# Adjacency build of a four-layer graph kernel: two edge tiles share one accumulator bank and a window of 20 destinations

## Chip, cores and metric

The kernel runs on one core of one Trainium2 chip. The metric is the device time of one execution in microseconds (us). Three runs of the kernel before took 2306.53, 2307.1 and 2308.04 us, median 2307.1 us.

## What is computed

The reference is a stack of four graph layers on 3125 nodes of 128 features. 53125 directed edges (`src`, `dst`) are sorted by destination. The first layer is the one that the change serves: four rounds of "add the neighbours, then a two-layer perceptron".

```python
for l in range(N_LAYERS):                                   # 4 rounds
    agg = jax.ops.segment_sum(x[src], dst, num_segments=n)  # sum over incoming edges
    h = x + agg
    h = jnp.maximum(h @ W1[l] + b1[l], 0.0)
    x = h @ W2[l] + b2[l]
...
x = _layernorm(x + _L0_gnn_ref(x, edge_index, batch0, ...), axis=-1)
x = _layernorm(x + _L1_gnn_ref(x, edge_index, edge_type_8, ...), axis=-1)
x = _layernorm(x + _L2_gnn_ref(x, edge_index, edge_type_16, ...), axis=-1)
x = _layernorm(x + _L3_gnn_ref(x, ..., src, dst, edge_type_8), axis=-1)
```

The other three layers gather rows by edge and sum them by relation; the change does not touch them.

## The kernel before

The kernel has four stages. A setup reads the edge lists and turns them into keys. The **adjacency build** makes a dense matrix `adj` of 128 partitions x 25 blocks x 3136 columns in bf16: row (block h, partition p) is source node 128h + p, a column is a destination, a cell counts edges. The four rounds of the first layer then multiply the node rows by this matrix (line 1320). Three passes with row gathers follow.

The build runs over 416 tiles of 128 edges, in 104 groups of four (`FG` = 4), four groups in a ring of buffers (`FNB` = 4).

- VectorE (DVE) makes for each group one one-hot of the source's place in its block, `flo` (line 2033, 128 x 512 for four tiles), and for each tile one one-hot `foh` (line 2037) of 800 columns: two sub-blocks of 16 destinations, each 25 source blocks x 16.
- TensorE (PE) multiplies the two for each tile, once for either sub-block (lines 1210 and 1212, 400 columns each). The product adds to an accumulator bank of 512 columns in `acc` that belongs to that sub-block of 16 destinations; which bank it is comes from a table read into registers.
- ScalarE (ACT) copies a finished pair of sub-blocks (32 destinations, two banks) into `adj` (line 1713, 128 x 800) and then writes zeros into the two banks (line 1717), since every product only adds. There are 98 pairs and three slots of two banks. How many tiles a pair waits for is data; ACT reads these counts into registers, 12 at a time (line 1719, the loop of line 1726).

The order between the engines is set by semaphores. `foh_ready` counts groups that DVE has made, `fstep_done` tiles that PE has multiplied, `flushed` pairs copied, `zeroed` pairs zeroed. PE waits for `foh_ready` and, by the pair that a group reaches, for `zeroed`; DVE waits for `fstep_done` before it overwrites a buffer; ACT waits for `fstep_done` before a copy and for its own `flushed` before it zeroes. After the build DVE adds the diagonal (lines 2053 and 2058), PE waits for `flushed`, `zeroed` and `diag_set`, and the first round begins (line 1320).

GpSimd (POOL) runs checks and tables in the setup (lines 893 to 931) and nothing during the build. The checks end in one number, `peak`: above 0 the kernel takes a general branch instead of the dense one.

Of the kernel before, what the change touches and what calls it, by code (L numbers as in the profile page):

```python
# [18 lines left out]
BF16 = mybir.dt.bfloat16  # L19
I32 = mybir.dt.int32  # L20
I16 = mybir.dt.int16
# [60 lines left out]
FSTEPS = FIT * FG * FNB  # L82
AHEAD = FG * FNB
FCOLS = BLOCKS * FB
PAIRS = FBLOCKS // 2
FSLOTS = 3
TURN = 4 * FSLOTS
COUNT_MAX = 255
COUNT_MASK = 1023
# [12 lines left out]
assert max(TILES, PAIRS) <= COUNT_MASK and FSTEPS == TILES  # L102
assert all(f * 171 >> 10 == f // (2 * FSLOTS) for f in range(FBLOCKS + 1))
# [49 lines left out]
def gnn(nc, x, src, dst, ea1, ea2, et16, et8, g0w1, g0b1, g0w2, g0b2, g1w, g1root, g1bias,  # L153
        g2w, g2comp, g2aw1, g2ab1, g2aw2, g2ab2, g2upd, g3w, g3bias, g3gw, g3gb, g3loop, out):
    with ExitStack() as ctx:
# [25 lines left out]
        adj = sb("adj", [P, BLOCKS, NA], BF16)  # L181
# [3 lines left out]
        def carve(shape, dt=F32):  # L185
# [5 lines left out]
            assert used[0] + words <= BLOCKS * NA // 2  # L191
# [28 lines left out]
        LOWA = -(-used[0] * 2 // NA)  # L220
# [17 lines left out]
        LOWB = -(-used[0] * 2 // NA)  # L238
# [46 lines left out]
        assert used[0] <= BLOCKS * NA // 2  # L285
# [12 lines left out]
        ends_m = carve([TQ, TC, PAIRS], BF16)  # L298
        key_q = carve([TQ, TW])
        ends_at = carve([TQ, TC])  # L300
        step_io = carve([P, WSTEPS])
        IW = WSTEPS + P + TC + 1 + 2 * FCOLS
        iota_i = carve([P, IW], I32)
        LATE = PAIRS * 2 * FB // 2 - 2 * WSTEPS

        def late_columns(b):
            o = b * NA // 2 + LATE
            return big[:, o:o + 2 * WSTEPS]

        turn_i = late_columns(BLOCKS - 1)[0:1, :].bitcast(I32).rearrange("p (k s) -> p k s", k=2)  # L310
        turn_f = late_columns(BLOCKS - 2)[0:1, :].rearrange("p (k s) -> p k s", k=2)
        bs_f, ts_f = (late_columns(BLOCKS - 3)[:, k * WSTEPS:(k + 1) * WSTEPS] for k in range(2))
        check_out = late_columns(BLOCKS - 4)[0:1, 0:CHECKW + 3 + FIT * FNB]
        assert CHECKW + 3 + FIT * FNB <= 2 * WSTEPS
# [7 lines left out]
        first_i = carve([1, TILES], I32)  # L322
        turn_q = carve([1, 2, TILES], I32)
        turn_w = carve([1, TILES // FG])
        fine_f = carve([1, TILES, 2])
        six_i = carve([1, 2, TILES, 2], I32)
        slot_f = carve([1, TILES, 2])
        assert used[0] <= (BLOCKS - 4) * NA // 2 + LATE and 2 * FB * TURN <= 2 * LATE

# [24 lines left out]
        o1 = FNB * FG * FCOLS  # L354
        o2 = o1 + FNB * FG * P // 2
        foh = feat[:, 0:o1].bitcast(BF16).rearrange("p (g j k) -> p g j k", g=FNB, j=FG)
# [7 lines left out]
        t1 = FSTEPS * 2  # L364
        t2 = t1 + FIT * FNB
        t3 = t2 + TILES // 2
        t4 = t3 + FCOLS

        temp = sb("temp", [P, max(3 * KB, t4)])
# [3 lines left out]
        fplace_i = temp[0:1, 0:t1].bitcast(I32).rearrange("p (g w) -> p g w", g=FIT * FNB // 2)  # L373
        fturn_i = temp[0:1, t1:t2].bitcast(I32).rearrange("p (i w) -> p i w", i=FIT)
        col_io = temp[:, t3:t4].bitcast(I16)
# [3 lines left out]
        flow = temp[:, t2:t3].bitcast(BF16)  # L379
# [9 lines left out]
        ends_i = sb("ends_i", [1, P], I32)  # L389
# [32 lines left out]
        fslots = [acc[:, i * 2 * KB:(i + 1) * 2 * KB].rearrange("p (k c) -> p k c", k=2)[:, :, 0:FCOLS]  # L422
                  for i in range(FSLOTS)]
# [64 lines left out]
        zeroed = sem("zeroed")  # L488
# [184 lines left out]
        def _(sp):  # L673
# [21 lines left out]

            sp.dma_start(firsts_i, every_tile(0, TILES)).then_inc(ends_in, 16)
# [9 lines left out]
            sp.wait_ge(flushed, PAIRS)  # L706
# [161 lines left out]
        def _(pool):  # L868
            o = 0
            for w, pat, cm in ((WSTEPS, [[1, WSTEPS]], 0), (P, [[1, P]], 0), (TC, [[1, TC]], TC),  # L870
                               (1, [[1, 1]], 1), (2 * FCOLS, [[1, 2 * FCOLS]], 0)):
                nc.gpsimd.iota(iota_i[:, o:o + w], pattern=pat, base=0, channel_multiplier=cm).then_inc(iota_set, 1)
                o += w
# [1825 lines left out]
```

## Time and profile before

| | us |
|---|---|
| time, median of three runs | 2307.1 (2306.53 to 2308.04) |
| profiled execution, span of its instructions (no other time of it is given) | 2719.1 |
| of it: setup, to the build's first DVE instruction | 0 to 40.8 |
| of it: build, to the first round's first matmul | 40.8 to 276.0 |
| of it: four rounds (line 1320) | 276 to 709 |
| of it: passes with gathers | 709 to 2719 |

The profiled execution is 412 us longer than the timed ones. A line L1713 is line 1713 of the kernel above. Each engine has one queue of instructions, worked off in order; a wait stops what stands behind it on that engine. The busy time of an engine is no bound by itself: what counts in the build is which engine the others wait for.

### The profile page before, as it was taken

Reading aid. Unit: us, or ns where it says so; the run is one execution under the profiler, and the core shown is the slowest. Engines: PE = TensorE matmul, PEld = TensorE weight load, DVE = VectorE, ACT = ScalarE, POOL = GpSimd, SP = SyncE. Lnnn points to the kernel's source line nnn. Section 1 sums busy time; section 2 is a strip of 40 time slices with the busy share of each in tenths; the row PEclk is TensorE's granted clock in tenths of the full one; section 3 lists DMA queues with packets and bytes.
Section 4 is the critical chain, followed back from the end, with each engine's and each line's share of the span. In section 5 each row is a group of like instructions: output and inputs, shape, how many; then the busy total and the mean of one; then the engine's idle time right before and its main releaser. Section 6 shows DMA issues by size and latency. Waiting matters only on the chain.

```text
span 2719.1 us, 32229 instructions
## 1 busy us (share of the span) xinstructions
PE 1467.8 (54%) x7630; PEld 1028.2 (38%) x7755; DVE 939.2 (35%) x2174; ACT 630.7 (23%) x1678; POOL 1356.5 (50%) x1567
## 2 busy tenths in 40 slices
PE   5666999999626666655774243333334323232233
PEld 3444454454425555444553132322323223232232
DVE  9877221226513333323343332332333212121122
ACT  3777000000112232222331233333334000000000
POOL 4000167500256555554533666666665566666664
PEclk9999999999768787777787666767667655665566
DMA  1000011002312222222222122222222211111111
GB/s 26 0 0 5 16 11 10 6 1 49 86 42 77 76 90 76 83 75 67 73 85 74 45 67 63 65 66 68 60 66 67 52 48 46 50 47 47 49 48 39
DMA packets 126215, 137.46 MB, mean 51 GB/s; under 512 B 80273, under 2 KB 97433, under 8 KB 123000
## 3 DMA queue, kind: packets, MB, share of 16 engines
q0 software_dynamic: 40896, 81.94, 12.0%
q1 hardware_dynamic: 85240, 54.54, 6.6%
q8 instruction: 40, 0.66, 0.1%
q14 instruction: 39, 0.32, 0.0%
HBM read 91.88 MB, written 44.52 MB: 50 GB/s over the span
## 4 chain that ended last, share of the span: by engine, by line
PE 36%; another core or an unknown queue 26%; issue 23%; DVE 9%; ACT 4%; DVEq 1%; POOL 1%; ACTq 0%; DMA 0%; POOLq 0%; SPq 0%
PE acc L1320 15%; PE acc L1591 6%; PE acc L1518 6%; PE acc L1488 5%; DVE feat L2037 1%; ACT adj L1789 1%; DVE adj L2025 1%; PE acc L1210 1%; PE acc L1212 1%; ACT adj L1713 1%; ACT acc L1717 1%; PE misc L1256 1%; POOL adj L1002 1%; DVE adj L2374 1%
## 5 line engine op out<-in xcount | busy, mean ns | idle before, releaser
L1002 POOL DMA_INDIRECT adj<-table,adj x832 | 792.0, 952 | 476.8 <-issue 241.0
L1002 POOL DMA_INDIRECT adj<-tablex,adj x416 | 392.8, 944 | 366.1 <-ACT adj L1766 166.7
L1591 PE MATMUL acc<-adj 128*128 x1760 | 329.2, 352 | 453.1 <-issue 247.8
L1591 PEld LDWEIGHTS acc<-adj 128*128 128x128 f32 x1760 | 298.9, 259 | 438.0 <-issue 437.5
L1320 PE MATMUL acc<-adj,feat 128*128 (+2 forms) x2031 | 401.3, 353 | 13.2 <-issue 9.4
L1518 PE MATMUL acc<-adj 128*128 128x128 f32 x1664 | 259.6, 320 | 79.8 <-issue 58.7
L1518 PEld LDWEIGHTS acc<-adj 128*128 128x128 f32 x1664 | 247.4, 232 | 116.0 <-issue 115.7
L2025 DVE TENSOR_TENSOR adj<-acc,drel 128x768 f32<-128x768 f32 (+1 forms) x148 | 138.4, 945 | 414.9 <-remote 285.4
L1320 PEld LDWEIGHTS acc<-adj,feat 128*128 (+1 forms) x2100 | 185.9, 98 | 217.5 <-issue 13.4
L1789 ACT ACTIVATE adj<-adj 128x128 f32<-128x128 f32 x832 | 261.9, 388 | 22.4 <-DVEq L2628 18.6
L1464 PE MATMUL acc<-ident,adj 128*128 128x128 f32 x48 | 21.6, 450 | 435.4 <-issue 327.4
L948 POOL TENSOR_TENSOR node_rep<-node_rep,compb 128x128 f32<-128x128 f32 x128 | 58.6, 458 | 328.6 <-DMA node_rep<-in_L_gnn_weight_dram 318.9
L1488 PE MATMUL acc<-adj 128*128 128x512 f32 (+2 forms) x400 | 187.9, 611 | 55.8 <-issue 28.9
L1210 PE MATMUL acc<-feat 128*128 128x400 bf16 x416 | 140.1, 337 | 74.0 <-ACT acc L1717 32.6
L1464 PEld LDWEIGHTS acc<-ident,adj 128*128 128x128 f32 x48 | 8.5, 178 | 445.1 <-issue 333.9
L2374 DVE TENSOR_TENSOR adj<-misc,adj 128x512 f32<-128x512 f32 x196 | 129.6, 716 | 88.5 <-PE acc L1518 48.9
L2448 DVE TENSOR_TENSOR adj<-acc,adj 128x128 f32<-128x128 f32 x50 | 14.5, 290 | 395.4 <-remote 355.2
L2037 DVE TENSOR_SCALAR feat<-temp,feat 128x800 bf16<-128x800 int16 x416 | 149.1, 421 | 0.0
L1766 ACT ACTIVATE adj<-feat 128x4 int32 (+1 forms) x98 | 17.1, 202 | 526.3 <-remote 413.3
L1212 PE MATMUL acc<-feat 128*128 128x400 bf16 x416 | 138.3, 332 | 0.0
L1488 PEld LDWEIGHTS acc<-adj 128*128 128x128 f32 x400 | 81.2, 243 | 110.8 <-issue 82.6
L1766 ACT ACTIVATE adj<-tile 128x4 int32 (+1 forms) x98 | 17.5, 202 | 349.8 <-remote 283.8
(351 smaller groups left out, 1425.3 us busy)
## 6 DMA issues: line engine op xcount, KB each, us to landing
table<-adj SPq DMA_DIRECT2D x24, 1024.0 KB
adj<-table,adj POOLq DMA_INDIRECT x834, 2.2
table<-adj SPq DMA_DIRECT2D x25, 512.0 KB
adj<-tablex,adj POOLq DMA_INDIRECT x416
table<-adj SPq DMA_DIRECT2D x25, 64.0 KB
out_dram<-adj SPq DMA_DIRECT2D x24, 64.0 KB
temp<-in_x_dram SPq DMA_DIRECT2D x4, 256.0 KB, 3.3
wrel<-node_rep SPq DMA_DIRECT2D x16, 64.0 KB
```

The costliest lines, as they stand in the source:

```text
L948: nc.gpsimd.tensor_tensor(sl_tmp if b else sl_out, of_b, by, ALU.mult).then_inc(slice_step, 1)
L1002: pool.indirect_dma_start(ring[:, p_, 0:D], None, rows_, bass.IndirectOffsetOnAxis(ap=gidx[:, p_:p_ + 1], axis=0)).then_inc(msgs_in[third_ ...
L1210: nc.tensor.matmul(acc[:, bass.ds(places[at_], FCOLS)], flo[:, q, :, j], foh[:, q, j, 0:FCOLS], start=False, stop=True, skip_group_check=True)
L1212: nc.tensor.matmul(acc[:, bass.ds(places[at_ + 1], FCOLS)], flo[:, q, :, j], foh[:, q, j, FCOLS:2 * FCOLS], start=False, stop=True, skip_g ...
L1320: last = nc.tensor.matmul(acc[:, c * KB:c * KB + chunk(c)], x3[:, s, bass.ds(b, 1), :].rearrange("p b f -> p (b f)"), adj[:, bass.ds(b, 1) ...
L1488: nc.tensor.matmul(o, xT1[:, b.r, :], table, start=True, stop=True).then_inc(prod_full[j], 1)
L1518: last = nc.tensor.matmul(acc[:, bass.ds(blk[2 * j + w], P)], ring[:, place_of(1, t, c) + j, 0:D], hot1[:, hot_slot(t, k), z, w * P:(w + 1 ...
L1591: last = nc.tensor.matmul(acc[:, bass.ds(blk[s], width)], hot[:, c, j, :], ring_flat[:, bass.ds(place[s], width)], start=False, stop=True, ...
L1789: last = nc.scalar.activation(o, o, ACT.Copy, scale=WEIGHT[ph][:, bass.ds(tiles_from(u, c) + j, 1)])
L2025: return nc.vector.tensor_tensor(o, numbers.unsqueeze(1).to_broadcast([P, n, P]), drel[:, bass.ds(s, n)].unsqueeze(2).to_broadcast([P, n, ...
L2037: last = nc.vector.tensor_scalar(foh[:, q, j, :], col_io, fkey[:, bass.ds(k * AHEAD + q * FG + j, 1)], None, ALU.is_equal)
L2374: nc.vector.tensor_tensor(hot1[:, hot_slot(t, k), 0:n_, :], kind_ps.unsqueeze(1).to_broadcast([P, n_, WIDE]), key1[:, bass.ds(t.num(TPT, j ...
```

## The change

- Two tiles (256 edges) form a **window**: 20 destinations that begin at the first destination of the window's first tile, whatever column that is. 416 tiles make 208 windows. Each window has one bank of 500 columns: 25 source blocks x 20 destinations. Banks are taken in turn, four of them (`FBANKS`).
- PE multiplies a window in three steps: the second tile over all 500 columns, which begins the bank anew (so nothing is zeroed any more); the first tile into 12 of each 20 columns (300 columns, in runs of 12); and the second tile of the window before into the first column of each 20 (25 columns, a step of 20), for the edges of the shared first destination. The bank is a constant of the program and no longer read from a table.
- DVE makes, for a group of four tiles, `flo` as before, two one-hots of 300 and two of 500 columns instead of four of 800, and one of 50 columns for the shared destinations.
- ACT makes one copy of 500 columns for a window into `adj` at the window's first destination (read into a register, 16 at a time), after its own copy before has ended, since neighbouring copies overlap. The zeroing goes.
- `adj` becomes 3144 columns wide. In the setup DVE loses the tables of places and waits and gains the keys of the 25-column step; POOL gains seven checks of windows; SP issues three more small loads ahead of those it had. ACT's first copy now waits for POOL's last table (`places_set`, 6), as all but the first 12 pairs did before. The diagonal of the first 24 blocks waits for 205 of 208 windows.

The core of the diff:

```diff
-            pe.wait_ge(walk_set, 2)
-            for b in (1, 2, 3, 4, 5, 0):
...
-                nc.tensor.matmul(acc[:, b * KB:(b + 1) * KB], zerob[:, 0:P], zerob[:, :], start=True, stop=True)
...
             with pe.Fori(0, FIT) as k:
...
-                    pe.wait_ge(zeroed, turns_[q] & COUNT_MASK)
-                    for j in range(FG):
-                        at_ = 2 * (q % 2 * FG + j)
-                        nc.tensor.matmul(acc[:, bass.ds(places[at_], FCOLS)], flo[:, q, :, j], foh[:, q, j, 0:FCOLS],
+                    for w in range(WPG):
+                        bank = ((q * WPG + w) % FBANKS) * KB
+                        pe.wait_ge(flushed, k * AHEAD + (q * WPG + w + 1))
+                        odd, even = 2 * w + 1, 2 * w
+                        nc.tensor.matmul(acc[:, bank:bank + WCOLS], flo[:, q, :, odd], foh[:, q, FOH_AT[odd]:FOH_AT[odd] + WCOLS],
+                                         start=True, stop=True, skip_group_check=True)
+                        window = acc[:, bank:bank + WCOLS].rearrange("p (h n) -> p h n", n=WN)
+                        nc.tensor.matmul(window[:, :, 0:WN_EVEN], flo[:, q, :, even],
+                                         foh[:, q, FOH_AT[even]:FOH_AT[even] + WCOLS_EVEN].rearrange("p (h n) -> p h n", n=WN_EVEN),
                                          start=False, stop=True, skip_group_check=True)
-                        nc.tensor.matmul(acc[:, bass.ds(places[at_ + 1], FCOLS)], flo[:, q, :, j], foh[:, q, j, FCOLS:2 * FCOLS],
+                        g, before = (q, odd - 2) if w else ((q - 1) % FNB, FG - 1)
+                        o = FOH_PIECES + (before // 2) * BLOCKS
+                        nc.tensor.matmul(window[:, :, 0], flo[:, g, :, before], foh[:, g, o:o + BLOCKS],
                                          start=False, stop=True, skip_group_check=True).then_inc(fstep_done, 1)
...
-            def copy_out(i, r, end):
-                hold(act, fstep_done, (end & COUNT_MASK) + AHEAD)
-                nc.scalar.activation(adj[:, :, bass.ds(i * (TURN * 2 * FB) + r * 2 * FB, 2 * FB)].rearrange("p h (k n) -> p h k n", k=2),
-                                     fslots[r % FSLOTS].rearrange("p k (h n) -> p h k n", n=FB), ACT.Copy).then_inc(flushed, 1)
-
-                hold(act, flushed, i * TURN + (r + 1))
-                nc.scalar.activation(fslots[r % FSLOTS], zerob[:, 0:FCOLS].unsqueeze(1).to_broadcast([P, 2, FCOLS]), ACT.Copy).then_inc(zeroed, 1)
...
+            with act.Fori(0, WINDOWS // WIN_TURN) as i:
+                _, bases = nc.values_load_multi_w_load_instructions(
+                    bases_i[0:1, bass.ds(i * WIN_TURN, WIN_TURN)], engines=[mybir.EngineType.Activation],
...
+                for r in range(WIN_TURN):
+                    bank = (r % FBANKS) * KB
+                    hold(act, fstep_done, i * WIN_TURN + (AHEAD + r + 1))
+                    hold(act, flushed, i * WIN_TURN + (FBANKS + r))
+                    nc.scalar.activation(adj[:, :, bass.ds(bases[r], WN)], acc[:, bank:bank + WCOLS].rearrange("p (h n) -> p h n", h=BLOCKS),
+                                         ACT.Copy).then_inc(flushed, 1)
...
                 for q in range(FNB):
-                    dve.wait_ge(fstep_done, k * AHEAD + (q + 1) * FG)
+                    dve.wait_ge(fstep_done, k * AHEAD + (q * WPG + 3))
...
                     for j in range(FG):
-                        last = nc.vector.tensor_scalar(foh[:, q, j, :], col_io, fkey[:, bass.ds(k * AHEAD + q * FG + j, 1)], None,
-                                                       ALU.is_equal)
-                    last.then_inc(foh_ready, 1)
+                        n_ = WN if j % 2 else WN_EVEN
+                        nc.vector.tensor_scalar(foh[:, q, FOH_AT[j]:FOH_AT[j] + n_ * BLOCKS].rearrange("p (h n) -> p h n", n=n_),
+                                                col_io.rearrange("p (h n) -> p h n", n=WN)[:, :, 0:n_], fkey[:, bass.ds(k * (FNB * FG) + q * FG + j, 1)], None,
+                                                ALU.is_equal)
+                    nc.vector.tensor_tensor(foh[:, q, FOH_PIECES:FOH_PIECES + WPG * BLOCKS].rearrange("p (w h) -> p w h", w=WPG),
...
-            dve.wait_ge(flushed, (BLOCKS - 1) * P // (2 * FB))
+            dve.wait_ge(flushed, EARLY_WINDOWS + FBANKS)
```

ACT in the loop of copies, before: one pair and the turn of the loop (`adj<-acc` is the copy, `acc<-zerob` the zeroing, an ISA row works out an address, `TENSOR_LOAD` reads the counts).

```order
L1713 ISA [waits fstep_done]
L1713 ACTIVATE adj<-acc 128x25x32
L574 REGISTER_ALU
L1717 ACTIVATE acc<-zerob 128x2x400 [waits flushed]
L1726 REGISTER_ALU
L1726 COMPARE_AND_BRANCH
L1719 TENSOR_LOAD ends_i
```

A pair is a copy and a zeroing, each of 800 columns, and a turn of the loop loads 12 counts.

ACT now: the head of the loop with its load of 16 first destinations, and the first window of 16.

```order
L1708 UNCONDITIONAL_BRANCH [waits ends_in,places_set,checks_set,ends_ready]
L1708 ISA
L1709 TENSOR_LOAD feat
L568 REGISTER_ALU
L568 REGISTER_ALU [waits fstep_done]
L1716 ISA [waits flushed]
L1716 ACTIVATE adj<-acc 128x25x20
```

The zeroing is gone, a copy has 500 columns, its address step stands behind the wait for the copy ahead of it, and the first copy stands behind `places_set`.

DVE in the loop of groups, before: the head of the loop, `flo`, and the first of four one-hots (`node_rep` holds the places, `temp` the column numbers and keys).

```order
L2030 UNCONDITIONAL_BRANCH [waits un_ps]
L2030 ISA
L2033 ISA [waits fstep_done]
L2033 TENSOR_TENSOR feat<-node_rep,temp 128x512
L2037 ISA
L2037 TENSOR_SCALAR feat<-temp,feat 128x800
```

Each group is one instruction of 512 columns and four of 800.

DVE now: the second window of a group, behind `flo` and the first window's two one-hots, and the end of the group.

```order
L2015 ISA
L2015 TENSOR_SCALAR feat<-temp,feat 128x300
L2015 ISA
L2015 TENSOR_SCALAR feat<-temp,feat 128x500
L2018 ISA
L2018 TENSOR_TENSOR feat<-temp 128x50
L2009 REGISTER_ALU
```

Four one-hots of 800 columns became two of 300 and two of 500, and one of 50 came in behind them.

## Rows read from the trace of the kernel before

**Rows 1.** Engines in 120 to 160 us: length, busy us (instructions) PE, PEld, DVE, ACT, POOL; clock, DMA, GB/s.

```profile
120.00:160.00 40.00, 26.60 (x145) 16.46 (x146) 31.81 (x93) 27.67 (x34) 0.00 (x0) 1.00 0.00 0
```

**Rows 2.** Waits from 40 to 276 us: who, for whom, us in total, times, longest.

```profile
ACT adj L1713 <- PE acc L1212: 58.7, 54, 5.8
DVE feat L2033 <- PE acc L1212: 36.8, 35, 1.6
PE acc L1210 <- ACT acc L1717: 32.6, 29, 1.8
...
PE acc L1210 <- DVE feat L2037: 14.9, 18, 1.9
```

**Rows 3.** Timeline of ACT in the build: start us, us, engine, line, operation [idle before].

```profile
202.24 0.84 ACT L1713 ACTIVATE adj<-acc 128x800 f32 x1 [0.83 <-PE acc L1212]
203.17 0.84 ACT L1717 ACTIVATE acc<-zerob 128x800 f32<-128x800 bf16 x1
204.84 0.84 ACT L1713 ACTIVATE adj<-acc 128x800 f32 x1 [0.83 <-PE acc L1212]
...
210.69 0.84 ACT L1717 ACTIVATE acc<-zerob 128x800 f32<-128x800 bf16 x1 [0.18 <-ACT adj L1713]
212.18 0.84 ACT L1713 ACTIVATE adj<-acc 128x800 f32 x1 [0.65 <-PE acc L1212]
```

**Rows 4.** Groups of ACT by shape, whole span: busy us, mean ns | idle before.

```profile
L1713 ACT ACTIVATE adj<-acc 128x800 f32 x84 | 69.8, 831 | 46.8 <-PE acc L1212 45.7 <-issue 0.4
...
L1811 ACT ACTIVATE adj<-acc 128x512 f32<-128x512 f32 x50 | 29.5, 596 | 107.3 <-PE acc L1488 55.5 <-issue 33.1 <-remote 18.2
...
L1697 ACT ACTIVATE tile<-misc 128x416 int16<-128x416 f32 x1 | 1.1, 1088 | 10.5 <-PE misc L1155 10.5
```

**Rows 5.** ACT's own queue at lines 1719 and 1713: ns least/median/most, first and last start.

```profile
L1719 ACTq TENSOR_LOAD <-ends_i x9: 288/785/990, 40.9 to 265.6; - x9
...
L1713 ACTq FUSED_REGOPS  x84: 46/46/52, 72.9 to 264.4; - x84
```

**Rows 6.** Timeline of DVE at the build's first groups.

```profile
40.82 0.40 DVE L2033 TENSOR_TENSOR feat<-node_rep,temp 128x512 bf16<-128x512 bf16 x1
41.15 1.42 DVE L2037 TENSOR_SCALAR feat<-temp,feat 128x800 bf16<-128x800 int16 x4
42.50 0.41 DVE L2033 TENSOR_TENSOR feat<-node_rep,temp 128x512 bf16<-128x512 bf16 x1
```

**Rows 7.** Timeline of PE: matmuls of 400 columns in the build, of 104 in the setup.

```profile
121.68 0.33 PE L1212 MATMUL acc<-feat 128*128 128x400 bf16 x1
121.85 0.33 PE L1210 MATMUL acc<-feat 128*128 128x400 bf16 x1
...
25.45 0.29 PE L1154 MATMUL misc<-adj 104*128 104x104 bf16 x1
25.53 0.29 PE L1155 MATMUL misc<-adj 104*128 104x104 bf16 x1
```

**Rows 8.** Timeline of POOL in the setup.

```profile
11.36 0.99 POOL L893 CAST adj<-adj 1x416 f32<-1x416 int32 x1 [5.14 <-DMA adj<-in_dst_dram]
...
22.76 1.64 POOL L912 TENSOR_SCALAR adj<-adj 1x450 int32<-1x450 f32 x1 [4.00 <-DVE adj L1974]
...
33.97 1.40 POOL L927 TENSOR_TENSOR adj<-adj 1x450 f32<-1x450 f32 x1 [1.69 <-ACT adj L1701]
...
38.02 1.94 POOL L931 TENSOR_SCALAR walk_i<-adj 1x450 int32<-1x450 f32 x1
```

**Rows 9.** Timeline of the build's end.

```profile
265.33 3.36 DVE L2053 TENSOR_TENSOR adj<-adj,ident 128x3072 bf16<-128x3072 bf16 x1 [3.88 <-ACT adj L1713]
...
268.78 0.82 ACT L1713 ACTIVATE adj<-acc 128x800 bf16<-128x800 f32 x1
...
269.69 0.84 ACT L1717 ACTIVATE acc<-zerob 128x800 f32<-128x800 bf16 x1
...
276.03 1.49 PE L1320 MATMUL acc<-adj,feat 128*128 128x512 bf16 x3 [8.03 <-issue]
```

More of the change, by code:

```diff
@@ L81 @@
 FIT = TILES // (FG * FNB)
[L82 to L87, printed above, removed]
+WINDOWS = TILES // 2
+WPG = FG // 2
+FBANKS = 4
+AHEAD = FNB * WPG
+WN, WN_EVEN, SPAN = 20, 12, 11
+WCOLS, WCOLS_EVEN = WN * BLOCKS, WN_EVEN * BLOCKS
+NAP = NA + 8
+FOH_AT, FOH_PIECES, FOH = (0, 304, 808, 1112), 1616, 1680
+TAIL_AT, TAIL_FIRST = NA - 16, NA - 16 - WN
+EARLY_WINDOWS = WINDOWS - 3
+WIN_TURN = 16
 COUNT_MAX = 255
+ENDS_IN = 6 * 16
 COUNT_MASK = 1023
@@ L101 @@
 CHECKW = 25 + 24 + TILES
-assert max(TILES, PAIRS) <= COUNT_MASK and FSTEPS == TILES
-assert all(f * 171 >> 10 == f // (2 * FSLOTS) for f in range(FBLOCKS + 1))
+assert TILES <= COUNT_MASK and FIT * FG * FNB == TILES and WINDOWS % WIN_TURN == 0 and WCOLS <= 512
+assert N - 1 + WN <= NAP and FOH_AT[1] >= WCOLS_EVEN and FOH_AT[3] + WCOLS <= FOH_PIECES and FOH_PIECES + WPG * BLOCKS <= FOH
 assert TQ * TC == TILES and WIDE == 2 * FB * R1 and TURNS == BLOCKS and (BLOCKS - 1) * P < NA <= NP
@@ L297, in gnn @@
         sel_m = carve([TQ, TC, STEPS], BF16)
-        ends_m = carve([TQ, TC, PAIRS], BF16)
         key_q = carve([TQ, TW])
-        ends_at = carve([TQ, TC])
+        piece_q = carve([TQ, WPG, P])
+        next_i = carve([TQ, WPG], I32)
+        next_f = carve([TQ, WPG])
         step_io = carve([P, WSTEPS])
-        IW = WSTEPS + P + TC + 1 + 2 * FCOLS
+        IW = WSTEPS + P + TC + 1 + WCOLS
         iota_i = carve([P, IW], I32)
[L304 to L314, printed above, removed]
         edge_i = carve([1, 2, WSTEPS + SPT], I32)
@@ L321, in gnn @@
         firsts_f, lasts_f = carve([1, TILES]), carve([1, TILES])
[L322 to L328, printed above, removed]
+        assert used[0] <= BLOCKS * NAP // 2
         feat = sb("feat", [P, NP + PARTS3 * NP // 2])
@@ L884, in _ @@
                 o += n
[L885 removed]
+            nc.gpsimd.iota(check_i[0:1, o:CHECKW], pattern=[[0, TILES]], base=SPAN, channel_multiplier=0).then_inc(checks_set, 1)
             pool.wait_ge(checks_set, 3)
@@ L1137, in _ @@
                 nc.tensor.transpose(acc[:, KB + c * TQ:KB + (c + 1) * TQ], key_q[:, c * P:(c + 1) * P], ident[0:TQ, 0:TQ])
-            for c in range(TC):
-                nc.tensor.matmul(acc[0:1, 5 * KB + 384:5 * KB + 384 + PAIRS], ones_b[:, 0:1], ends_m[:, c, :], start=(c == 0), stop=(c == TC - 1))
+            for c in range(WPG):
+                nc.tensor.transpose(acc[:, 5 * KB + c * TQ:5 * KB + (c + 1) * TQ], piece_q[:, c, :], ident[0:TQ, 0:TQ])
             pe.wait_ge(idents_set, len(SCALES))
@@ L1216, in _ @@
-            pe.wait_ge(zeroed, FSLOTS + PAIRS)
+            pe.wait_ge(flushed, WINDOWS + FBANKS)
             pe.wait_ge(diag_set, 1)
@@ L1718, in load_ends @@
-            def load_ends(i, n):
-                _, ends = nc.values_load_multi_w_load_instructions(
-                    ends_i[0:1, bass.ds(i * TURN, n)], engines=[mybir.EngineType.Activation],
-                    min_val=0, max_val=FSTEPS, skip_runtime_bounds_check_because="a number of steps")
-                return ends
-            for r, end in enumerate(load_ends(0, TURN)):
-                copy_out(0, r, end)
-            act.wait_ge(places_set, 6)
-            with act.Fori(1, PAIRS // TURN) as i:
-                for r, end in enumerate(load_ends(i, TURN)):
-                    copy_out(i, r, end)
@@ L1934, in _ @@
             o = 0
-            for t, w in ((step_io, WSTEPS), (node_io, P), (tile_io, TC), (part_io, 1), (col_io, 2 * FCOLS)):
+            for t, w in ((step_io, WSTEPS), (node_io, P), (tile_io, TC), (part_io, 1), (col_io, WCOLS)):
                 link(nc.vector.tensor_copy(t[:, :], iota_i[:, o:o + w]))
```

150 lines of the change are left out of this document (73 added, 77 removed).

## The prediction

> **What bounds the kernel now.** I read the stage table first. In 40 us of the build PE is busy for 26.6, DVE for 31.8 and ACT for 27.7 us, POOL for none, at a granted clock of 1.00 [rows 1]: no engine is full, so the build is bound by waits. The list of waits says whose: ACT's copy waits 58.7 us for PE, DVE 36.8 us for PE, and PE 32.6 us for ACT's zeroing against 14.9 us for DVE [rows 2]. ACT and PE take turns. The timeline shows one turn: a copy at 202.24, the zeroing at 203.17, then 0.83 us in which ACT waits until PE has worked on in the zeroed banks, the next copy at 204.84 [rows 3]. That is 2.60 us a pair where ACT works for 1.68. DVE alone would be faster: its first groups, which nothing holds, start 1.68 us apart (40.82 and 42.50) [rows 6], which is 175 us for 104 groups; the build takes 235 us from its first DVE instruction to the first round's first matmul at 276.03 [rows 6, 9].
>
> **Removed, added and moved.** The change takes the zeroing out, so the turn-taking goes: PE needs only a bank that was copied four windows earlier. Three engines could set the pace instead. I cost each for one window of two tiles.
>
> *ACT.* The copy of 800 columns takes 831 ns, a copy of 512 columns 596 [rows 4]; the difference is 0.82 ns a column, so 500 columns take 0.59 us. A copy now waits for the one ahead of it. The nearest row of such a wait is the zeroing behind its own copy: it starts 0.93 us after it, 0.09 behind its end [rows 3]. The address step then stands behind the wait; it takes 46 ns [rows 5], and I give it 0.07 with its issue. A window costs 0.59 + 0.09 + 0.07 = 0.75 us, 208 windows 156 us. At each turn of the loop ACT loads registers. A load of 12 takes 785 ns, the one at the end, of a single register, 288 [rows 5]: 45 ns a register, 0.96 us for 16. From the last copy before a turn to the next copy it is 1.49 us now (210.69 to 212.18) [rows 3]; of that 0.70 is not the load, so 1.66 us with 16 registers, 0.91 more than a usual window. Twelve turns cost 11 us. **ACT: 167 us**, 0.80 a window.
>
> *DVE.* `flo` stays: 0.33 us to the next instruction; the four one-hots of 800 share the other 1.35 of the 1.68, 0.34 each [rows 6]. Of the 0.34 I take 0.13 as fixed, an estimate, and 0.26 ns a column for the rest: 0.26 us for 500 columns, 0.21 for 300, and 0.13 for the 50. A group is 0.33 + 0.52 + 0.42 + 0.13 = 1.40 us, 104 groups 146 us. The bounds: no one-hot gets dearer per column (0.21 and 0.13 us, no fixed part): 1.13 us a group, 118 us in all. Or the one-hots of 300, which read runs of 12, fall to one column in 1.09 ns, the rate of the diagonal (3072 columns in 3.36 us [rows 9]): 0.13 + 0.33 = 0.46 each, 1.90 us a group, 198 us. The nearest row is line 2037's own, the same operation on the same operands, so I take 1.40.
>
> What the Trainium skill says of such runs: "Vector Engine (DVE) Microarchitecture Reference", section 5.1, has a one-source operation on 2-byte data at four a cycle only where the outermost counts of input and output are even or equal, else at two. The 25 runs read and the single run of 300 written are neither; by that, as an estimate, a 300 costs 0.29 us and a group 1.56, or 162 us for the build. No row of before shows such runs; this makes the DVE rival below likelier than the row of 800 does, and I have set its chance with that in mind.
>
> *PE.* Matmuls of 400 columns follow each other in 0.17 us, 0.42 ns a column; those of 104, each with its own weights, in 0.08 to 0.09 [rows 7]. A window is 0.21 + 0.13 + 0.09 = 0.43 us, 89 us in all. PE is ahead of both.
>
> So ACT sets the pace, with DVE 21 us behind it. With four banks and 3.5 groups of one-hots between them, what is late next is nothing until one of the two is dearer than I take it.
>
> *The start.* ACT may not copy before POOL's last table, which ends at 39.96 [rows 8]. POOL waits 5.14 us for loads, 4.00 for DVE and 1.69 for ACT's answer [rows 8]. Four of the seven checks are on 208 numbers, half of the cast's 416 with 0.99 us [rows 8], and three on a single one: about 3 us as an estimate. The three small loads ahead have no row; I take 2 us, between nothing and the 5.14 of the present wait. The wait for DVE swallows 4.00 of these 5. ACT's answer comes earlier, since DVE reaches its part without the tables removed ahead of it, so the 1.69 goes. POOL ends at about 39.96 + 1 - 1.7 = 39.3, and with the loop's first load (0.96, and 0.3 to reach the copy) the first copy starts at 40.5. DVE starts no later than now (40.82) and probably some 4 us earlier; if not, the first window comes 2 to 3 us after that point, and this goes into the range.
>
> *The end.* The last copy ends at 40.5 + 167 = 207.5. The diagonal (3.36 us [rows 9]) may start when 205 windows are copied, 2.25 us earlier: it ends 1.2 us behind the last copy, and its tail 0.25 later, at 209.0. PE starts line 1320 at 276.03 now, 5.50 behind the end of the last zeroing (269.69 + 0.84) [rows 9]; that stretch of waits and branches stays. So line 1320 starts at 214.5.
>
> **The sum.** 276.0 - 214.5 = 61.5 us. What follows is untouched, with the same waits among the same engines; a column stride of 3144 instead of 3136 has no price in any row, and I take none. All durations are from an execution of 2719.1 us, while the runs have a median of 2307.1. I carry the 61.5 us over whole, since the build moves no data by DMA [rows 1] and consists of instructions of fixed length: 2307.1 - 61.5 = **2245.6 us**. If the profile stretched everything alike (by 2719.1 / 2307.1 = 1.18), the saving would be 52 and the time 2255.
>
> **Rivals.**
>
> *DVE sets the pace (13%).* For it: the runs of 12, which nothing in the trace prices; DVE has the least idle time now [rows 1]. Against: it is the same operation. At the upper bound of 1.90 us a group from 37 us on, DVE ends at 235, the last copy 2 us later, line 1320 starts 7 behind that, at 244: saved 32, **2275 us**. It decides from 1.61 us a group on.
>
> *The matmuls into stepped columns are slow (5%).* The 300 and the 25 columns go to the bank in runs of 12 and at a step of 20; every matmul of before writes one run. The 500 stay whole. PE takes over only when a window is above 0.80 us, with 0.30 for the rest 1.5 ns a stepped column against 0.42; at four times the rate, 1.67, a window is 0.84 and the build 8 us longer: **2254 us**. A lower clock in the build acts the same way: at half the clock of rows 1 a window would be 0.7 to 0.85. The Trainium skill, "PSUM — Partial Sum Buffer", section Specifications (TRN2), says that any non-contiguous pattern slows matmuls significantly; it gives no factor, and no row here shows one.
>
> *ACT's copies to odd columns are slow: slower than before (5%).* A window begins at any column, so a run of 20 bf16 begins on an odd one in half the cases; before, every run of 32 began at a multiple of 32. One row shows ACT writing where it doesn't write whole runs: 416 columns of int16 at a step of four took 1088 ns [rows 4], with 0.17 fixed 2.2 ns a column. At that rate a copy is 1.27 us, a window 1.43, ACT 309 us, line 1320 starts at 356: **2387 us**. It turns slower than before from 1.04 us a window, a copy of 0.88, or 1.4 ns a column. Against it: copies in runs of 32 cost no more than 0.82 ns a column [rows 4], and a run of 20 is still a run. Half-way, at 1.0 ns a column, it is 19 us dearer: 2265.
>
> *It doesn't do what it says (2%).* If a check of windows fails, `peak` sends the kernel into its general branch; or all engines keep turn-taking over four banks. Then the time is at the old one or above.
>
> **Chances and range.** Forecast 75%, with 2236 to 2256 for itself (ACT at 0.71 or 0.80 a window, the start 3 us either way). The range that holds 8 in 10 goes from 2236 to 2275, which takes in the stretched profile, the stepped columns and DVE's upper bound. About 0.2% (4.6 us) is what a measurement of this kernel can tell from no change: faster by more 92%, within 2%, slower by more 6%.
>
> **What would show it.** Right: copies of 0.59 us, 0.75 apart; ACT idle before a copy only at the turns, 1.66 us; DVE and PE waiting for ACT; no zeroing; line 1320 starting near 214. DVE's steps: one-hots of 300 and 500 at 0.21 and 0.26 us apart. Wrong: ACT's copy waiting for PE with PE waiting for DVE (the DVE rival), copies well above 0.6 us (odd columns), matmuls of 300 columns above 0.13 us apart, or a first copy later than 44 us.

## The result, and the profile after

The changed kernel takes **2252.14 us** (median of four runs, 2251.02 to 2252.66) against 2307.48 us before (four runs, 2306.53 to 2308.04): a ratio of 0.976, 95% interval 0.9746 to 0.9773. The forecast was 2245.6 us with a range of 2236 to 2275. It was faster, by 55.3 us where 61.5 were forecast. The profiled execution of the changed kernel spans 2250.9 us, so this one isn't stretched as that of before was; only stretches of the build are compared below. The build of before was not stretched: in three edits of the old kernel below, whose profiled executions span 2254 to 2292 us, DVE's first group starts at 40.82 to 40.84 us, as it does before (40.82 [rows 6]).

The build's end tells the same sum. The first round (now line 1317) starts at 220.42 us instead of 276.03 [rows 9], 55.6 us earlier, and 55.3 came out: nothing was gained or lost behind the build. POOL's setup, and start and end of the build, from the timeline (start us, us, engine, line, operation, idle before):

```profile
14.57 0.52 POOL L894 CAST adj<-adj 1x416 f32<-1x416 int32 x1 [8.63 <-DMA adj<-in_dst_dram]
...
16.18 0.77 POOL L898 TENSOR_TENSOR temp<-adj 1x208 f32<-1x208 f32 x1
...
21.05 1.63 POOL L907 TENSOR_TENSOR adj<-adj 1x416 f32<-1x416 f32 x1
...
38.72 1.38 POOL L942 TENSOR_SCALAR walk_i<-feat 1x450 int32<-1x450 f32 x1
...
41.97 0.59 ACT L1716 ACTIVATE adj<-acc 128x500 f32 x1 [6.42 <-PE acc L1210]
...
213.68 0.66 ACT L1716 ACTIVATE adj<-acc 128x500 f32 x1 [0.16 <-ACT adj L1716]
...
220.42 7.77 PE L1317 MATMUL acc<-adj,feat 128*128 128x512 bf16 x24 [8.68 <-issue]
```

What paces the build now, from the list of waits between 40 and 214 us (who, for whom, us in total, times, longest):

```profile
...
PE acc L1202 <- ACT adj L1716: 43.3, 147, 1.3
ACT adj L1716 <- ACT adj L1716: 27.4, 174, 0.2
ACT adj L1716 <- PE acc L1210: 23.7, 34, 6.4
...
DVE feat L2010 <- PE acc L1210: 9.2, 17, 1.2
PE acc L1202 <- DVE feat L2018: 5.1, 3, 4.5
```

PE waits for ACT, DVE in turn for PE, and ACT mostly for its own copy ahead. That is the forecast's picture: ACT sets the pace. Beside rows 2, ACT's 58.7 us for PE are down to 23.7; the loop's twelve turns (14.0 us) and the start (6.42 us) are most of these, since a turn's load of registers is put down to PE, which had long been done. ACT's timeline across one turn:

```profile
105.41 0.59 ACT L1716 ACTIVATE adj<-acc 128x500 f32 x1 [0.16 <-ACT adj L1716]
106.15 0.59 ACT L1716 ACTIVATE adj<-acc 128x500 f32 x1 [0.16 <-ACT adj L1716]
106.90 0.68 ACT L1716 ACTIVATE adj<-acc 128x500 f32 x1 [0.16 <-ACT adj L1716]
108.67 0.59 ACT L1716 ACTIVATE adj<-acc 128x500 f32 x1 [1.09 <-PE acc L1210]
```

Copies of 0.59 us, 0.75 apart, and 1.77 at the turn (its idle time of 1.09 us is the shortest of the twelve, the longest is 1.21); but the third copy takes 0.68. The groups by shape (busy us, mean ns | idle before) show that the mean copy is 614 ns, and that DVE's one-hots of 300 columns are dearer than those of 500; one group of DVE from its timeline takes 1.53 us from `flo` to `flo`:

```profile
L1716 ACT ACTIVATE adj<-acc 128x500 f32 x208 | 127.6, 614 | 51.1 <-ACT adj L1716 27.4 <-PE acc L1210 23.7
...
L2015 DVE TENSOR_SCALAR feat<-temp,feat 128x300 bf16<-128x300 int16 x208 | 75.8, 364 | 0.0
L2015 DVE TENSOR_SCALAR feat<-temp,feat 128x500 bf16<-128x500 int16 x208 | 71.4, 343 | 0.0
```

```profile
39.51 0.41 DVE L2010 TENSOR_TENSOR feat<-node_rep,temp 128x512 bf16<-128x512 bf16 x1
...
39.84 1.15 DVE L2015 TENSOR_SCALAR feat<-temp,feat 128x300 bf16<-128x300 int16 x4
...
41.04 0.41 DVE L2010 TENSOR_TENSOR feat<-node_rep,temp 128x512 bf16<-128x512 bf16 x1
```

PE's windows, at the higher clock (195.68; the next steps start 0.23 and then 0.13 us later) and at the lower one (from the start of the build), and the table of stages, whose granted clock fell from 1.00 [rows 1] to 0.87:

```profile
195.68 0.40 PE L1202 MATMUL acc<-feat 128*128 128x500 bf16 x1 [0.19 <-ACT adj L1716]
...
195.91 0.29 PE L1205 MATMUL acc<-feat 128*128 128x300 bf16 x1
...
196.04 0.19 PE L1210 MATMUL acc<-feat 128*128 128x25 bf16 x1
```

```profile
41.25 0.60 PE L1202 MATMUL acc<-feat 128*128 128x500 bf16 x1
...
41.64 0.46 PE L1205 MATMUL acc<-feat 128*128 128x300 bf16 x1
...
41.96 0.59 PE L1202 MATMUL acc<-feat 128*128 128x500 bf16 x1
```

```profile
120.00:160.00 40.00, 29.71 (x145) 13.08 (x146) 37.73 (x146) 29.38 (x49) 0.00 (x0) 0.87 0.00 0
```

### The profile page after: what moved, and what is told of

Read it like the earlier page. It is cut to its first block, busy times and chain, and to the rows that moved or that the text cites. A ratio compares the mean times of both kernels' runs of the same rounds, so it can differ in the third digit from the quotient of the medians.

```text
span 2250.9 us, 31616 instructions
## 1 busy us (share of the span) xinstructions
PE 1480.2 (66%) x7538; PEld 1002.9 (45%) x7539; DVE 914.6 (41%) x2269; ACT 601.0 (27%) x1689; POOL 1360.9 (60%) x1574
## 4 chain that ended last, share of the span: by engine, by line
POOL 50%; PE 21%; issue 18%; ACT 5%; DVE 2%; ACTq 1%; DMA 1%; POOLq 1%; SPq 0%; DVEq 0%
POOL adj L1013 50%; PE acc L1317 18%; ACT adj L1716 5%; PE misc L1253 1%; PE acc L1202 1%; ACTq L1709 1%; DMA adj<-table,adj 1%; DVE adj L2610 0%; PE acc L1588 0%; DVE adj L2609 0%; PE acc L1205 0%; ACTq L1716 0%; POOLq L1009 0%; PE acc L1253 0%; POOLq L1010 0%
## 5 line engine op out<-in xcount | busy, mean ns | idle before, releaser
L1588 PE MATMUL acc<-adj 128*128 x1760 | 367.3, 387 | 494.3 <-DMA adj<-table,adj 249.4
L1588 PEld LDWEIGHTS acc<-adj 128*128 128x128 f32 x1760 | 330.6, 286 | 555.9 <-issue 555.9
L1317 PE MATMUL acc<-adj,feat 128*128 (+1 forms) x2100 | 406.3, 354 | 8.8 <-issue 8.7
L1515 PE MATMUL acc<-adj 128*128 128x128 f32 x1664 | 253.2, 317 | 113.1 <-ACT adj L1775 94.8
L1515 PEld LDWEIGHTS acc<-adj 128*128 128x128 f32 x1664 | 237.5, 227 | 154.2 <-issue 154.0
L1716 ACT ACTIVATE adj<-acc 128x500 f32 x208 | 127.6, 614 | 51.1 <-ACT adj L1716 27.4
L1202 PE MATMUL acc<-feat 128*128 128x500 bf16 x208 | 94.4, 454 | 49.2 <-ACT adj L1716 43.3
L2015 DVE TENSOR_SCALAR feat<-temp,feat 128x300 bf16<-128x300 int16 (+1 forms) x416 | 120.5, 354 | 0.0
L1485 PEld LDWEIGHTS acc<-adj 128*128 128x128 f32 x400 | 79.4, 238 | 91.3 <-issue 50.8
L1736 ACT ACTIVATE feat<-acc,l0c 128x512 f32<-128x512 f32 (+1 forms) x28 | 15.6, 634 | 342.7 <-PE acc L1317 342.7
L1205 PE MATMUL acc<-feat 128*128 128x300 bf16 x208 | 68.8, 331 | 0.0
L1202 PEld LDWEIGHTS acc<-feat 128*128 128x128 bf16 x208 | 23.6, 114 | 91.8 <-ACT adj L1716 86.2
```

The costliest lines, as they stand in the source:

```text
L1202: nc.tensor.matmul(acc[:, bank:bank + WCOLS], flo[:, q, :, odd], foh[:, q, FOH_AT[odd]:FOH_AT[odd] + WCOLS], start=True, stop=True, skip_g ...
L1205: nc.tensor.matmul(window[:, :, 0:WN_EVEN], flo[:, q, :, even], foh[:, q, FOH_AT[even]:FOH_AT[even] + WCOLS_EVEN].rearrange("p (h n) -> p ...
L1317: last = nc.tensor.matmul(acc[:, c * KB:c * KB + chunk(c)], x3[:, s, bass.ds(b, 1), :].rearrange("p b f -> p (b f)"), adj[:, bass.ds(b, 1) ...
L1485: nc.tensor.matmul(o, xT1[:, b.r, :], table, start=True, stop=True).then_inc(prod_full[j], 1)
L1515: last = nc.tensor.matmul(acc[:, bass.ds(blk[2 * j + w], P)], ring[:, place_of(1, t, c) + j, 0:D], hot1[:, hot_slot(t, k), z, w * P:(w + 1 ...
L1588: last = nc.tensor.matmul(acc[:, bass.ds(blk[s], width)], hot[:, c, j, :], ring_flat[:, bass.ds(place[s], width)], start=False, stop=True, ...
```

## Experiments: what held the build before

The prediction's account of the old kernel was that copy and zeroing kept ACT and PE in turns. Three runs of the kernel before take its causes apart.

**The zeroing alone taken out.**

```diff
-                nc.scalar.activation(fslots[r % FSLOTS], zerob[:, 0:FCOLS]..., ACT.Copy).then_inc(zeroed, 1)
+                act.sem_inc(zeroed, 1)
```

> The kernel before, with the zeroing instruction alone taken out; all waits stay (the banks are then reported as zeroed without being so, the sums add up over stale banks). Theory, the taking of turns between copy and zeroing held the build: DVE sets the pace with its 1.68 us a group, 104 groups are 175 us where the build took 235, line 1320 starts near 222 us instead of 276, the time is about 2254 us, so that the zeroing alone is worth what the whole change brought. Rival, three slots and the waits for data keep ACT and PE in turns without the zeroing: DVE goes on waiting for PE, the time stays above 2285 us.

Measured: 2293.93 us, ratio 0.994 (0.9925 to 0.9956). 14 us, not 53: the theory fell. The waits of this run:

```profile
ACT adj L1713 <- PE acc L1212: 136.0, 98, 7.1
PEld acc L1210 <- issue: 85.6, 63, 2.8
```

ACT now waits for PE before each of its 98 copies, and PE's weight loads stand idle for 85.6 us behind "issue", time in which they wait for nothing that the profile shows. In PE's own queue lie the loads of the places (line 1202), which can fill such time; here they are in the kernel before (ns least/median/most), with the row of its list of waits that goes with them and that rows 2 left out:

```profile
L1202 PEldq TENSOR_LOAD <-temp x52: 1100/1104/1125, 40.7 to 262.3; - x52
```

```profile
PEld acc L1210 <- issue: 100.0, 71, 2.4
```

52 loads of 1.10 us and 26 of 0.33 for the counts are 66 us of PE's queue in the build of 235. Two groups take PE up to 16 x 0.17 us of matmuls [rows 7], 1.10 and half of 0.33 for loads, 4.0 us in all, where DVE takes 3.4 [rows 6]: so PE stays the slower of the two without the zeroing.

**PE's tables taken out, zeroing kept, and both taken out.** PE's loop is written out, 104 groups with constants in place of what it read.

```diff
-            with pe.Fori(0, FIT) as k:
-                _, turns_ = nc.values_load_multi_w_load_instructions(fturn_i[...], ...)
-                        _, places = nc.values_load_multi_w_load_instructions(fplace_i[...], ...)
+            for n in range(FIT * FNB):
...
-                        nc.tensor.matmul(acc[:, bass.ds(places[at_], FCOLS)], ...)
+                    nc.tensor.matmul(acc[:, a:a + FCOLS], ...)
```

> The kernel before, with the zeroing, but PE reads no table: the 104 groups are written out one behind the other and the bank of each product and the count to wait for are constants (the numbers that this input's destinations give). In the run without zeroing PE still stood idle for 85.6 us with no other engine to wait for; its queue loads 16 places for two groups in 1.10 us and 4 counts in 0.33, 66.7 us in all, and spends a step of its own on each matmul's address. Theory, PE's loads and the zeroing together held the build: without the loads ACT's own work of a copy and a zeroing sets the pace, 98 pairs at about 1.9 us and 8 turns at 0.65 are 190 us, line 1320 starts near 236, the time is about 2268 us. Rival, the zeroing is what holds it and the loads only lie in its shade: the time stays above 2290 us.

> As the run before it, and without the zeroing (the sums add up over stale banks). Theory: neither holds the build any more, DVE's 1.68 us a group is left, 175 us, line 1320 near 222, about 2254 us, which is what the whole change brought. Rival, the three slots or the granularity of the waits hold it as well: above 2270 us.

Measured: 2273.67 us (ratio 0.9852, 0.9837 to 0.9867) without the tables, 2256.6 us (0.9782, 0.9767 to 0.9797) without either. Against 2307.8 us of the kernel before, measured beside them, that is 34.1 and 51.2 us; the zeroing alone had been 14, and 34.1 + 13.9 = 48.0. So the two are about additive, PE's queue is the larger by more than two to one, and together they nearly make up the whole change. The waits of the run without tables:

```profile
PEld acc L1201 <- issue: 44.1, 64, 1.5
PE acc L1201 <- ACT acc L1708: 33.5, 83, 1.2
ACT adj L1704 <- PE acc L1203: 26.6, 27, 6.8
```

and of the run without either, with the stage from 120 to 160 us of its build:

```profile
...
PEld acc L1201 <- DVE feat L2028: 56.2, 104, 2.1
```

```profile
120.00:160.00 40.00, 36.50 (x191) 19.73 (x191) 40.00 (x120) 19.18 (x23) 0.00 (x0) 1.00 0.00 1
```

Without tables PE waits for the zeroing (line 1708) as the prediction had it; without either PE waits for DVE once in each of the 104 groups, and DVE is busy for 40.00 of 40 us, at 1.68 us a group. The row of "issue" is not loads alone: without any load 44.1 of its 100.0 us are left, and 0.5 without the zeroing as well. What these runs don't part is the loads of the tables from the step that each matmul's address took from a register and from the turns of PE's loop: all went together. Both runs have this input's numbers written into the program, so they explain the old kernel and could not replace it.

## Experiments: what paces it now

**Two banks instead of four** (`FBANKS = 2`).

> The changed kernel with two banks in turn instead of four. Theory, ACT sets the pace and PE needs 0.43 us a window, so a bank that comes free while ACT copies the other one is filled in time: the time stays within 5 us of 2252, a little above it where the granted clock is at its lower level and a window takes PE 0.72 us. Rival, the number of banks is what decouples PE and ACT: with two they take turns again, a window is 0.75 + 0.5 us, the build over 100 us longer, the time near 2350 us.

Measured: 2265.79 us, 13.7 above the changed kernel. Neither number: no taking of turns, but more than 5 us. The timeline at the lower clock shows where (PE's step of 500 columns and ACT's copy, starting 0.8 to 1.0 us apart; ACT waits 0.41 for PE), and the stage's clock (0.69 here, 0.87 to 0.91 with four banks):

```profile
88.96 0.61 PE L1202 MATMUL acc<-feat 128*128 128x500 bf16 x1
89.31 0.59 ACT L1716 ACTIVATE adj<-acc 128x500 f32 x1 [0.41 <-PE acc L1210]
...
89.95 0.60 PE L1202 MATMUL acc<-feat 128*128 128x500 bf16 x1
```

```profile
160.00:200.00 40.00, 32.35 (x132) 12.30 (x130) 34.99 (x132) 26.72 (x43) 0.00 (x0) 0.69 0.00 0
```

The mechanism was the theory's (a window of 0.72 us of PE and the steps between the engines no longer fit into one copy at the lower clock); its size was taken from the clock with four banks, and with two the lower clock came more often. ACT's idle time between copies is 13.4 us longer than with four banks, and 12.6 of that lie in stretches at the lower clock.

**The bank read from a table again**, in the changed kernel.

```diff
+                    if q % 2 == 0:
+                        _, places = nc.values_load_multi_w_load_instructions(banks_i[0:1, 0:16], ...)
...
-                        bank = ((q * WPG + w) % FBANKS) * KB
+                        bank = places[(q * WPG + w) % FBANKS]
```

> The changed kernel, with the bank of each window read from a table again: PE loads 16 registers for every two groups, and each matmul's address is worked out from a register. Theory, PE's loads cost 1.1 us of its queue for four windows: a window takes PE 0.43 + 0.3 = 0.73 us at the higher clock and about 1.0 at the lower one, where ACT has 0.80; the stretches at the lower clock become PE's, some 10 to 25 us on the build, 2262 to 2277 us. Rival, four banks cover it: within 2 us of 2252.

Measured: 2252.23 us, the changed kernel's time. The loads are there, and cost nothing:

```profile
L1199 PEldq TENSOR_LOAD <-banks_i x52: 1102/1104/1299, 34.1 to 208.1; - x52
```

For four windows PE needs 4 x 0.44 + 1.1 = 2.9 us at the higher clock, ACT 3.2 us, and with filled banks ahead ACT doesn't notice a gap of 1.1 us. The rival was right. What cost 34 us in the old kernel is hidden in the new one: there PE had 16 matmuls of 400 columns for two groups, 2.7 us, beside the load, and ACT had to hand a bank back between. So it was not the constant bank that brought the 34 us to the changed kernel: beside the load PE has less to do, 1.8 us for eight tiles instead of 2.7.

**Single loads, and the contiguous source.** Two edits of the changed kernel, apart and together: ACT loads the next window's first destination behind each copy instead of 16 ahead of a turn; DVE's one-hots of 300 read a table of 300 in one run.

```diff
-                _, bases = nc.values_load_multi_w_load_instructions(bases_i[0:1, bass.ds(i * WIN_TURN, WIN_TURN)], ...)
+                base = base_of(0)
...
+                    if r + 1 < WIN_TURN:
+                        base = base_of(r + 1)
```

```diff
-                                                col_io.rearrange("p (h n) -> p h n", n=WN)[:, :, 0:n_], fkey...
+                                                col_io if j % 2 else col_even[:, :], fkey...
```

> ACT loads the first destinations one at a time, each behind the copy before it, and only the first of a turn ahead of the copies (16 at once now, 1.02 us in which no copy runs). Theory, ACT sets the pace: the single loads fit beside the copies, whose pitch stays at 0.75 us; a turn costs 0.3 us above a usual window where it cost 1.02, the build is some 9 us shorter, the time about 2243 us. Rival, DVE sets the pace: DVE needs 1.53 us a group, 0.765 a window, whatever ACT does, and only what DVE waits for now (9 us in all) could come back; PE waits for DVE instead of ACT and the time stays above 2248 us. Rival, the loads don't fit beside a copy: the pitch grows above 0.75 us and the time does not fall.

> DVE's one-hots of 300 columns read a table of their own, 300 in one run, instead of 12 out of each 20. Theory on DVE, reading in runs of 12 is what makes a 300 as dear as a 500 (364 against 343 ns): the 300 falls to about 0.24 us, a group from 1.53 to about 1.33 us. Rival on DVE: the length has little to do with the price, and the 300 stays above 0.3 us. Theory on the pace, ACT sets it: DVE only waits longer, the time stays within 2 us of 2252. Rival, DVE sets it: 0.2 us a group off 104 groups, about 2232 us.

> Both edits at once: single loads and the contiguous source. ACT sets the pace: the time of the single loads alone, about 2243 us, within 2 us. If DVE held back the single loads: the two together bring more than the sum, below 2240 us.

Measured: 2243.09, 2251.39 and 2242.34 us. ACT sets the pace in all three: its single loads are worth 9 us; DVE's new source is worth under 1 us, with the single loads or without, which is within the spread of the runs. A turn with single loads leaves 0.35 us before a copy where it left 1.09 (0.35 to 0.49 over the twelve turns, where it was 1.09 to 1.21):

```profile
104.35 0.60 ACT L1719 ACTIVATE adj<-acc 128x500 f32 x1 [0.35 <-ACT adj L1719]
105.10 0.66 ACT L1719 ACTIVATE adj<-acc 128x500 f32 x1 [0.16 <-ACT adj L1719]
```

And DVE did get faster with the contiguous source, 0.21 us from a 300 to the next instruction instead of 0.28, 1.39 us a group; it only waited longer:

```profile
60.53 0.43 DVE L2013 TENSOR_TENSOR feat<-node_rep,temp 128x512 bf16<-128x512 bf16 x1
60.87 0.29 DVE L2018 TENSOR_SCALAR feat<-feat 128x300 bf16<-128x300 int16 x1
61.08 0.34 DVE L2018 TENSOR_SCALAR feat<-temp,feat 128x500 bf16<-128x500 int16 x1
...
61.92 0.42 DVE L2013 TENSOR_TENSOR feat<-node_rep,temp 128x512 bf16<-128x512 bf16 x1
```

**The wait for the copy ahead without an instruction of its own**, with the contiguous source and without it; both with single loads.

```diff
-                    hold(act, flushed, i * WIN_TURN + (FBANKS + r))
+                    act.wait_ge(flushed, i * WIN_TURN + (FBANKS + r))
```

> Both edits, and the wait for the copy ahead stands on the address step itself instead of on an instruction of its own before it (17 ns and 27 ns to the address step). ACT sets the pace: the gap between copies falls from 0.16 to about 0.11 us, 208 windows give 9 us, about 2234 us. Rival, PE or DVE sets the pace by then: the gap falls and the copies wait for PE, the time stays at that of both edits.

> Single loads and the wait on the address step, with the one-hots of 300 read in runs of 12 as in the changed kernel. Theory: DVE needs 1.53 us a group, 159 us from 37.8 on, and ACT about 155 from 41.0 on, so now DVE sets the pace and the last copy ends near 199 us instead of 196: about 2236.5 us, 3 above the same with the contiguous source. Rival, ACT still sets it: 2234 us.

Measured: 2233.91 us with the contiguous source, 2236.57 without it, both as expected. With the stepped source DVE has become the bound, as the waits and a stage of that run show (DVE busy 40.00 of 40 us, the clock back at 1.00):

```profile
...
PE acc L1202 <- DVE feat L2023: 48.0, 73, 4.5
PE acc L1202 <- ACT adj L1719: 16.3, 27, 0.6
```

```profile
120.00:160.00 40.00, 24.00 (x156) 13.75 (x156) 40.00 (x159) 32.17 (x53) 0.00 (x0) 1.00 0.00 0
```

DVE's 104 groups of 1.53 us are 159 us. ACT needs 172 in the changed kernel, 164 with single loads, and 155 with the shorter wait as well (in the run with the contiguous source), less than DVE. The 2233.91 us (ratio to before 0.9674, 0.9661 to 0.9687) is the fastest of all runs, 18 us below the changed kernel.

**Longer turns**: 52 windows in a turn instead of 16 on top of that, and the first copy ahead of the wait for POOL's last table.

> Single loads, the contiguous source and the wait on the address step, with 52 windows in a turn of ACT's loop instead of 16 and the first copy no longer behind the wait for POOL's last table. ACT sets the pace: 9 turns fewer at 0.3 us and a first copy 0.5 us earlier give 3 us, about 2231 us against 2234. Rival, DVE sets the pace at 1.39 us a group (0.695 a window against 0.705 for a copy): the copies wait for PE more often, the time stays at 2234 us.

Measured: 2240.18 us, 6.3 slower than the same with 16; neither theory had this. ACT stands still for 2.61 us at each of its three turns (a stretch of copies is one row). That is 7.8 us against 4.7 for twelve short turns; the rest of the 6.3 lies in eleven gaps of 0.23 to 0.30 us, some 22 windows apart and at the same places of every turn (ahead of its windows 6, 27 and 49, counted from 0). The cause of these is open:

```profile
77.47 2.15 ACT L1719 ACTIVATE adj<-acc 128x500 f32 x3 [0.29 <-ACT adj L1719]
82.23 2.09 ACT L1719 ACTIVATE adj<-acc 128x500 f32 x3 [2.61 <-issue]
...
86.75 15.11 ACT L1719 ACTIVATE adj<-acc 128x500 f32 x21 [0.30 <-PE acc L1212]
...
102.16 1.40 ACT L1719 ACTIVATE adj<-acc 128x500 f32 x2 [0.30 <-ACT adj L1719]
```

**Every copy one column further right.**

```diff
-                    nc.scalar.activation(adj[:, :, bass.ds(bases[r], WN)], ...
+                    nc.scalar.activation(adj[:, :, 1:NAP][:, :, bass.ds(bases[r], WN)], ...
```

> The changed kernel with every copy written one column further right (the matrix is off by one column, which the rounds then read). In the changed kernel 57 of 208 copies take 0.66 to 0.68 us and 151 about 0.59: those whose first column is 5 or 7 beyond a multiple of 8. Theory, the column at which a copy begins sets this: now the windows at 4 and 6 (45 of them) are the long ones, and those at 5 and 7 fall to 0.59 us; 12 long copies fewer are 1 us, the time about 2251 us. Rival, it is the window's data or the moment at which others work: the same 57 copies stay long.

The first windows begin at columns 0, 15, 29, 42, 56. Their copies in the changed kernel, then shifted by one:

```profile
42.72 0.68 ACT L1716 ACTIVATE adj<-acc 128x500 f32 x1 [0.16 <-ACT adj L1716]
43.56 0.67 ACT L1716 ACTIVATE adj<-acc 128x500 f32 x1 [0.16 <-ACT adj L1716]
```

```profile
42.70 0.59 ACT L1716 ACTIVATE adj<-acc 128x500 f32 x1 [0.17 <-ACT adj L1716]
43.46 0.60 ACT L1716 ACTIVATE adj<-acc 128x500 f32 x1 [0.17 <-ACT adj L1716]
```

Columns 15 and 29 (7 and 5 beyond a multiple of 8) cost 0.68 and 0.67 us, 16 and 30 cost 0.59 and 0.60. Over all copies the long ones move as the theory says: in the changed kernel the 57 at 5 and 7 take 657 to 685 ns and the other 151 587 to 603, here the 45 at 4 and 6 take 657 to 683 ns. The 1 us that this should have brought didn't show (2252.55 us): the idle time before a copy went from 0.16 to 0.17 us, which takes it back, and whose cause is open.

## Why the prediction was right, and where it wasn't

**ACT sets the pace: right.** The single loads and the shorter wait moved the time by what ACT's own queue gave up, 9 and 8 us; DVE's gain moved nothing.

**The sum, 6 us off.** Line 1317 started at 220.42 instead of 214.5. The start took 1.5 us of that: the first copy came at 41.97, not 40.5. POOL's last table ended at 40.10 instead of 39.3: the loads cost 3.2 us and not 2 (14.57 against 11.36 [rows 8]), the seven checks 4.9 and not 3 (16.18 to 21.05); the waits for DVE and ACT did go. That alone would have been 42.4; the rest of POOL's chain took 20.7 us instead of 22.9, which the forecast did not have and which hid most of the error. And the first load of registers took 1.23 us instead of 0.96. The copies took 4.9: they were busy for 127.6 us where 208 x 0.59 = 122.7 were put in, and 4.6 of it are the 57 long ones at 80 ns more. The idle time between them was hit: 44.7 us, against 33 for the windows and 11 for the turns. For the turns that was luck: the row behind their 1.66 us starts at a zeroing of 0.84 us (210.69 [rows 3]) and not at a copy, so with a copy's 0.59 it would have given 1.41, and 1.77 came. The end gave 0.9 back: 6.08 us from the last copy's end instead of 7.0. Carrying the 61.5 us over whole was right: the build was not stretched, and line 1317 moved by as much as the time did. That the stretched alternative, 2255 us, came out nearer is chance.

**Copies to odd columns, a rival at 5%.** Its mechanism is there and its size isn't: an eighth more (not double), and for two of the eight places (5 and 7), not for every odd one. This term should have been a few us in the sum and not a case of its own. The Trainium skill, "SBUF — State Buffer", section Specifications (TRN2), has lines of 16 bytes, 8 columns here, and asks for at least two hits in a line for full bandwidth. If `adj` begins on a line (its rows of 3144 columns are a multiple of 8), a run of 20 columns from place 5 has a single column in its last line, one from place 7 a single column in its first, and a run from any other place has two or more in each: the trace agrees, in the changed kernel and shifted by one. No run here changed the length of a run, so that this is the cause is not shown.

**DVE: the term was wrong, and the time didn't show it.** A 300 costs 0.28 us to the next instruction, not 0.21, a group 1.53, not 1.40; the 500 and the 50 came as forecast, at 0.26 and 0.12. The step that failed is "the nearest row is line 2037's own": that row reads one run. The Trainium skill, "Vector Engine (DVE) Microarchitecture Reference", section 5.1, has two columns a cycle instead of four for such a pair of shapes, which gave 0.29 and 1.56 as an estimate, and the trace agrees; the contiguous source, at 0.21, is what the row of 800 had promised. DVE was 13 us behind ACT (159 against 172), not 21.

**The matmuls into stepped columns: right to leave them out.** 300 columns in runs of 12 follow in 0.13 us at the higher clock, 0.43 ns a column, as the 400 in one run do [rows 7]. The significant slowing that the Trainium skill, "PSUM — Partial Sum Buffer", section Specifications (TRN2), has for such patterns did not appear in this case.

**What bounded the kernel before: wrong, by half.** The prediction put the whole loss on the taking of turns and dropped the row with 100.0 us of "issue" from its list. More than half of that row went with the tables that PE read into registers (44.1 us are left without them), and these were worth more than the zeroing (34 us against 14). The forecast came out all the same, because it was not made by subtracting the old loss, but by adding up what each engine would need in the new order; all that the account of the old kernel had to supply was where the build ended.

**The clock.** The forecast took 1.00 for PE and named the lower level as a danger: at half the clock 0.7 to 0.85 us a window. The build did run partly there (0.87 to 0.91), with 0.71 us a window (41.25 to 41.96). Four banks cover it; two don't, which cost 13.7 us.

## What to carry to other kernels

When a queue is idle behind "issue" for a large share of a stretch, look into that queue for loads of registers before naming another engine's work as the cause; here the tables behind it were worth 34 us, though not all of the row was theirs. For a new structure add up each engine's own row of instructions, waits and loads, and ask by how much the second is behind; an account of why the old one was slow isn't needed for it and may be half wrong. Small steps on the pacing engine's own queue (a load before a loop's turn, a wait with an instruction of its own) are worth their length times their count as long as the next engine is behind, and nothing from there on: 9 + 8 us here, the last 3 of them only with DVE made faster too.

## What the runs showed of the hardware

- A load of registers holds its queue for 0.28 us with one register and 1.02 with 16 on ACT, 0.33 with 4 and 1.10 with 16 on PE. With one load behind each copy the copies still started 0.75 us apart.
- A copy of 25 runs of 20 bf16 columns took 587 to 603 ns, but 657 to 685 ns where the run began 5 or 7 columns beyond a multiple of 8; shifted by one column, the long ones were those that then began there.
- A loop of ACT with 16 windows and single loads turned with 0.35 to 0.49 us before the next copy, one of 52 windows (some 310 instructions) with 2.61 us. The Trainium skill, "Advanced Engine Details and Errata", section ISA Cache, has lines of 256 instructions, two of them; the longer body no longer fits one and, depending on where it begins, may not fit two. That the 2.3 us are a load of instructions is not shown by these runs.
- The granted clock in the build was 1.00 before, 0.87 to 0.91 in the changed kernel and 0.69 to 0.88 with two banks. In the changed kernel it fell to the lower level behind eleven of ACT's twelve turns (0.50 from 204.9 to 208.2 us, behind a turn in which PE stood idle for 1.23 us, and 1.00 from 194.7 to 204.8); with single loads it was 1.00 from 44 to 204 us, with ACT still setting the pace. Idle time of PE alone does not explain it: before, PE stood idle for up to 1.8 us [rows 2] at 1.00. What it follows is open.
